# Attention on one core: values weighed one pair of units later, projections in the next group's first pairs, VectorE in another order

## What is computed

```python
def _L1_xattn_ref(x, context, Wq, Wk, Wv):
    q = x @ Wq.T
    k_raw = context @ Wk.T
    v_raw = context @ Wv.T
    ...
    q = _rmsnorm(q)
    k = _rmsnorm(k)
    scale = HEAD_DIM ** (-0.5)
    scores = jnp.einsum('bhnd,bhmd->bhnm', q, k) * scale
    attn = jax.nn.softmax(scores, axis=-1)
    out = jnp.einsum('bhnm,bhmd->bhnd', attn, v)
    return out.transpose(0, 2, 1, 3).reshape(b, n, NHEADS * HEAD_DIM)
...
x = x + jnp.tanh(g_xattn[1]) * _L1_xattn_ref(_layernorm(x, axis=-1), ctx_2048, L1_xattn_Wq, L1_xattn_Wk, L1_xattn_Wv)
x = x + jnp.tanh(g_ffn[1]) * _L1_ffn_ref(_layernorm(x, axis=-1), ...)
```

## Time and profile before

| | us |
|---|---|
| median of three runs (lowest, highest) | 1179.31 (1172.65, 1180.49) |
| the profiled execution, its own time | 1173.06 |
| its span, first to last instruction | 1171.2 |
| mean granted TensorE clock, share of full | 0.948 |
| PE busy | 984.8 |
| DVE busy | 695.1 |
| ACT busy | 670.7 |
| POOL busy | 505.5 |

### The profile page before, as it was taken

One profiled execution on the slowest core, in us unless ns is written; L12 is line 12 of the kernel. 1 busy time (PEld: TensorE's weight loads), 2 busy tenths in 40 slices (PEclk: granted clock), 3 DMA queues, 4 the chain that ended last, 5 costly groups with the idle time before them and its releaser, 6 DMA issues. The chain is left out here.

```text
span 1171.2 us, 27695 instructions
## 1 busy us (share of the span) xinstructions
PE 984.8 (84%) x9516; PEld 565.1 (48%) x9517; DVE 695.1 (59%) x1653; ACT 670.7 (57%) x1091; POOL 505.5 (43%) x442
## 2 busy tenths in 40 slices
PE   5889999969799799999879999974699898888840
PEld 2545656446576477776657777752122122111120
DVE  8686755578687453344333532214587787876677
ACT  4655655445343255565445644443778888899940
POOL 0222231157576345565545755542122354543422
PEclk9999999999899999999999999995899999999975
DMA  6534231389973377778676767657658889676211
GB/s 235 180 127 139 82 129 65 130 198 177 205 162 91 115 196 162 167 181 197 153 186 157 151 130 122 113 88 185 163 104 186 167 170 183 148 175 146 66 42 64
DMA packets 183636, 170.85 MB, mean 146 GB/s; under 512 B 137316, under 2 KB 138916, under 8 KB 182628
## 3 DMA queue, kind: packets, MB, share of 16 engines
q1 hardware_dynamic: 155698, 111.67, 38.4%
q0 software_dynamic: 25888, 56.43, 23.8%
q10 hardware_dynamic: 1954, 1.54, 0.5%
HBM read 80.87 MB, written 65.20 MB: 125 GB/s over the span
## 5 line engine op out<-in xcount | busy, mean ns | idle before, releaser
L2070 ACT ACTIVATE sb_atp<-ps_atpS 128x1024 f32<-128x1024 f32 x256 | 242.2, 1038 | 33.5 <-PE ps_atpS L1809 33.3
L1501 PEld LDWEIGHTS ps_shpH<-sb_roxT,sb_rowt 128*128 (+1 forms) x2844 | 169.0, 107 | 25.3 <-DVE sb_roxT L1361 6.7
L1501 PE MATMUL ps_shpH<-sb_roxT,sb_rowt 128*128 128x128 f16 (+1 forms) x2844 | 173.5, 220 | 6.4 <-DVE sb_roxT L1361 6.4
L1490 PE MATMUL ps_shpY<-sb_rowt,sb_rohhl 128*128 (+1 forms) x711 | 168.3, 382 | 0.5 <-DVE sb_rohhl L1366 0.4
L1821 PE MATMUL ps_atpO<-sb_atp,sb_atv 128*17 128x512 f32 x1024 | 135.6, 601 | 29.1 <-ACT sb_atp L2070 26.2
L1103 POOL DMA_INDIRECT sb_roxg<-xn,sb_roentry x79 | 81.8, 1036 | 122.1 <-DMA sb_roentry<-list 89.5
L1204 ACT ACTIVATE sb_roh<-ps_shpH,sb_rob 128x128 f32<-128x128 f32 (+1 forms) x237 | 68.9, 361 | 112.4 <-PE ps_shpH L1501 98.3
L1490 PEld LDWEIGHTS ps_shpY<-sb_rowt,sb_rohhl 128*128 128x128 f16 (+1 forms) x711 | 66.6, 98 | 67.6 <-issue 3.1
L1091 POOL DMA_INDIRECT list<-sb_shentry,sb_shposb x64 | 72.8, 1137 | 43.2 <-DVE sb_shposb L1276 26.3
L1193 ACT ACTIVATE sb_roy<-ps_shpY,sb_roentry 128x512 f32<-128x512 f32 x79 | 54.1, 685 | 65.2 <-PE ps_shpY L1490 45.6
L1113 POOL DMA_INDIRECT x2a<-sb_roy,sb_roentry x40 | 67.4, 1684 | 29.7 <-ACT sb_roy L1193 23.5
(11 more groups left out here) (354 smaller groups left out, 1769.7 us busy)
## 6 DMA issues: line engine op xcount, KB each, us to landing
sb_rowt<-rw SPq DMA_DIRECT2D x15, 768.0 KB
sb_rowt<-rw SPq DMA_DIRECT2D x15, 704.0 KB
kst<-sb_kykp SPq DMA_DIRECT2D x16, 512.0 KB
qst<-sb_quqp SPq DMA_DIRECT2D x12, 512.0 KB, 3.8
vst<-sb_kyvt SPq DMA_DIRECT2D x16, 272.0 KB
sb_atv<-vst SPq DMA_DIRECT2D x32, 136.0 KB
sb_stage<-ctxT SPq DMA_DIRECT2D x4, 1024.0 KB, 6.0
sb_shxin<-x SPq DMA_DIRECT2D x16, 256.0 KB
```

What stands on the lines that cost most here:

```text
L1490: last = e.matmul(pY[it.p][:, :], hhl[it.p][0:n, x, k * P:(k + 1) * P], weight(value, 2 * W1 + w + k * D, n, D), start=j == 0, stop=j == l ...
L1501: last = e.matmul(rpH[it.p][0:n, f * P:(f + 1) * P], weight(ex["up"], w + k * FF + f * P, P, n), rxT[it.p][:, x + k, :], start=j % (3 * KD ...
L2070: S.done(e.activation(pr[n % 6][:, :], pS[n % 3][:, :], ACT.Exp, scale=HD ** -0.5 / SA ** 2), "atexp")
```

## The change

The number of probability tiles `pr` goes from six to eight; the four tiles `xin`, which hold loaded rows before the first group, now lie in the first two `pr`, so that the SBUF used stays the same. TensorE weighs pair m-2 behind the scores of pair m, where it weighed pair m-1. A group's pairs 2 and 3 are therefore weighed in the next group, behind its scores of the pairs 0 and 1. Both halves of a projection now stand in group s+1, behind the scores of its pairs 0 and 1 and ahead of the `weigh` there. `turn` of the last group moves from behind `weigh` at pair 2 to ahead of `weigh` at pair 3. After the last group there are two `weigh` in place of one. On VectorE `projected`, `evacuate` and `normalise` move in each slot from behind `norm` to behind `choose` and `affine`, so that `scale`, `parts`, `spread`, `low`, `squares`, `scales` and `choose` of a slot come ahead of them; `roots` and `spread2` come behind them.

```diff
--- before.py
+++ after.py
@@ -1545,7 +1545,6 @@
         o = sb(mem, "o", [P, NT, D])
         x2 = sb(mem, "x2", [P, NT, D])
 
-        xin = [sb(mem, f"quxin{i}", [P, D]) for i in range(FIRST)]
         st, mv = [sb(mem, f"qust{i}", [P, 6]) for i in range(2)], [sb(mem, f"qumv{i}", [P, 2]) for i in range(2)]
         ve, rstd = ([sb(mem, f"qu{n}{i}", [P, 1]) for i in range(2)] for n in ("ve", "rstd"))
         rs = [sb(mem, f"qurs{i}", [P, 1]) for i in range(2)]
@@ -1562,7 +1561,9 @@
         q = [sb(mem, f"atq{i}", [P, 2, SEQ], f16) for i in range(3)]
         k = [sb(mem, f"atk{i}", [P, 2, SEQ], f16) for i in range(3)]
         vv = [sb(mem, f"atv{i}", [P, 4, 4 * (HD + 1)]) for i in range(3)]
-        pr = [sb(mem, f"atp{i}", [P, 2 * SEQ]) for i in range(6)]
+        NP_ = 8
+        pr = [sb(mem, f"atp{i}", [P, 2 * SEQ]) for i in range(NP_)]
+        xin = [pr[i // 2][:, i % 2 * D:(i % 2 + 1) * D] for i in range(FIRST)]
         oT = [sb(mem, f"atoT{i}", [P, SEQ]) for i in range(2)]
         rc = sb(mem, "atrc", [P, 4, 4])
         table = sb(mem, "attable", [P, 1])
@@ -1699,7 +1700,7 @@
                 r = slice(it.n * P, (it.n + 1) * P)
                 e.dma_start(x2[:, it.n, :], R["x2a"][r, :]).then_inc(S.sem(f"quxin{it.n}"), 16)
                 if it.n < FIRST:
-                    e.dma_start(xin[it.n][:, :], R["x1"][r, :]).then_inc(S.sem(f"quxin{it.n}"), 16)
+                    e.dma_start(xin[it.n], R["x1"][r, :]).then_inc(S.sem(f"quxin{it.n}"), 16)
 
             def turn(it):
                 S.reach(e, "quxl", it, it.n - FIRST + 1)
@@ -1819,7 +1820,7 @@
                 for i in range(4):
                     n = HD + 1
                     last = e.matmul(pO[it.p][32 * i:32 * i + n, :], vv[it.n % 3][:, m, i * n:(i + 1) * n],
-                                    pr[(it.n * 8 + 2 * m + i // 2) % 6][:, (i % 2) * SEQ:(i % 2 + 1) * SEQ], start=m == 0, stop=m == 3)
+                                    pr[(it.n * 8 + 2 * m + i // 2) % NP_][:, (i % 2) * SEQ:(i % 2 + 1) * SEQ], start=m == 0, stop=m == 3)
                 S.done(last, "atpv")
 
             def turn(it):
@@ -1873,17 +1874,16 @@
                     for m in range(4):
                         scores(it, 2 * m)
                         scores(it, 2 * m + 1)
-                        if m == 0 and it.n - 1 in started:
-                            project(started[it.n - 1], 6, 12)
-                        if m > 0:
-                            weigh(it, m - 1)
+                        if m < 2 and it.n - 1 in started:
+                            project(started[it.n - 1], 6 * m, 6 * m + 6)
+                        if m == 3 and it.n > 0:
+                            turn(it.back(1))
+                        if m > 1:
+                            weigh(it, m - 2)
                         elif it.n > 0:
-                            weigh(it.back(1), 3)
-                        if m == 2 and it.n > 0:
-                            turn(it.back(1))
-                        if m == 3 and it.n in started:
-                            project(started[it.n], 0, 6)
+                            weigh(it.back(1), m + 2)
                 if h == 2 * NG:
+                    weigh(It((NG - 1) // 2, 1), 2)
                     weigh(It((NG - 1) // 2, 1), 3)
                     turn(It((NG - 1) // 2, 1))
             e.wait_ge(S.sem("ato"), NG)
@@ -2065,9 +2065,9 @@
                 if n == 2:
                     for p in range(2):
                         S.wait_moved(e, "ququt", It(1, p))
-                if n >= 6:
-                    e.wait_ge(S.sem("atpv"), n // 2 - 2)
-                S.done(e.activation(pr[n % 6][:, :], pS[n % 3][:, :], ACT.Exp, scale=HD ** -0.5 / SA ** 2), "atexp")
+                if n >= NP_:
+                    e.wait_ge(S.sem("atpv"), (n - NP_) // 2 + 1)
+                S.done(e.activation(pr[n % NP_][:, :], pS[n % 3][:, :], ACT.Exp, scale=HD ** -0.5 / SA ** 2), "atexp")
 
             def signs(it):
                 S.wait(e, "law", it)
@@ -2151,7 +2151,7 @@
             def spread(it):
                 if it.n < FIRST:
                     v.wait_ge(S.sem(f"quxin{it.n}"), 32)
-                    line(v.tensor_tensor(x2[:, it.n, :], x2[:, it.n, :], xin[it.n][:, :], ALU.add))
+                    line(v.tensor_tensor(x2[:, it.n, :], x2[:, it.n, :], xin[it.n], ALU.add))
                 else:
                     v.wait_ge(S.sem(f"quxsum{it.n}"), 16)
                 line(v.bn_stats(st[it.p][:, :], x2[:, it.n, :]))
@@ -2329,12 +2329,6 @@
                         low(it)
                 for it in q_at(h, 2):
                     norm(it)
-                for it in g_at(h, 3):
-                    normalise(it)
-                for it in q_at(h, 6, FIRST):
-                    projected(it)
-                for it in g_at(h, 2):
-                    evacuate(it)
                 for it in n_at(h, 1):
                     scale(it)
                 for it in n_at(h, 2):
@@ -2345,19 +2339,25 @@
                     low(it)
                 for it in q_at(h, 7):
                     squares(it)
-                for i, at in n_slot.items():
-                    if at == h:
-                        roots(i)
                 for it in c_at(h, 2):
                     scales(it)
                 if h in inner_at:
                     chosen(inner_at[h])
                 for it in c_at(h, 4):
                     choose(it)
+                if h - 1 in inner_at:
+                    affine(inner_at[h - 1])
+                for it in q_at(h, 6, FIRST):
+                    projected(it)
+                for it in g_at(h, 2):
+                    evacuate(it)
+                for it in g_at(h, 3):
+                    normalise(it)
+                for i, at in n_slot.items():
+                    if at == h:
+                        roots(i)
                 for it in c_at(h, 1):
                     spread2(it)
-                if h - 1 in inner_at:
-                    affine(inner_at[h - 1])
                 if h - 2 in inner_at:
                     slices(inner_at[h - 2])
                 if h - 3 in inner_at:
```

## The result

| | before | after |
|---|---|---|
| median (lowest to highest), us | 1175.98 (1166.88 to 1180.49) | 1195.19 (1194.12 to 1197.45) |
| ratio, 95% interval | 1 | 1.015 (1.0114 to 1.0186) |
| profiled execution: span, us | 1171.2 | 1194.1 |
| mean granted TensorE clock | 0.948 | 0.933 |
| first to last exponential, us | 833.55 to 1116.34: 282.8 | 832.94 to 1139.04: 306.1 |

The changed kernel is 1.5% slower, some 19 us. The sum had said 4.4 us, so the side is right and the size is far off. The 1195.19 us lie above the forecast's own range (1175 to 1192) and just inside the wide one (1166 to 1196), and that is luck: the kernel before has a median of 1175.98 here and had 1179.31 in the forecast, where a ratio of 1.015 makes 1197.0. Within one per cent had the chance 0.61, and slower than that 0.23. All of the loss lies in the attention, which is 23.3 us longer in the profile.

What follows compares the result with a forecast made beforehand. TensorE was taken to bound groups with a projection, ScalarE the others. 1173.1 us less 15.7 of gains plus 20.1 of VectorE waits made 1177.5, or 1183.7 on the median's scale; range 1175 to 1192, eight in ten 1166 to 1196.

Steps and rivals of the forecast that it cites:

- The sum: Whole kernel: profiled 1173.1 us less 15.7 of gains plus 20.1 of losses, 4.4 us slower.
- Waits of groups 1 to 5: TensorE waits for `normalise` behind VectorE's new order in the early groups, together 10.8 us.
- The gain of 2.1 us: Groups 1 to 5: later weighing brings five groups to 9.50 us each, and group 1 starts 1.40 earlier.
- Groups 6 to 19: Two groups go from 18.01 to 17.1 us; late `normalise` costs waits of 1.5, 6.4 and 1.35 us.
- gains of 6.3 + 0.85: Middle groups: 0.9 us for each of seven pairs, 6.3, and a late transfer's 0.85 us counted as gone.
- about 1.5 of the signs': This stretch's part of the signs' waits for VectorE, 2.7 us in all, expected to go with `scales` earlier.
- Late groups: Groups 20 to 31, without projection: two take 15.22 us instead of 15.84, six pairs gain 3.7 us.
- The 0.22 and 0.98 gaps: ScalarE's usual idle gaps ahead of exponentials; their disappearance was named a sign of a right forecast.
- the gain of 15.7 us: Later weighing across the attention: gains of 3.7, 6.3, 2.7, 0.85 and 2.1 us together.
- A: Rival: VectorE is never late and the whole 15.7 us are gained, 1163.6 us; chance 0.18.
- B: Rival: TensorE's clock falls in the long waits for VectorE, 9.6 us more, 1193 us; chance 0.17.
- C: Rival: DMA engines bound the middle, bunching costs some 3 us, 1187 us; chance 0.05.

Runs made afterwards that it cites:

- e1: The changed kernel with the whole old order of steps on VectorE; 1185.21 us, ratio 1.0035 to the kernel before.
- e4: The changed kernel with `spread` alone moved behind `normalise` on VectorE; 1183.86 us, ratio 1.0037 to the kernel before.
- e12: The kernel of e6 without nine of the eleven steps of each `roots`; 1159.35 us, ratio 0.9938 to the kernel before.
- e9: The changed kernel with the old VectorE order, but `scales` ahead of `normalise`, and queries' transposes first in SyncE's queue; 1164.78 us, ratio 0.9983.
- e10: The kernel before, with its own weighing and six buffers, plus `scales` ahead of `normalise` and queries' transposes first in SyncE's queue; 1171.63 us, ratio 1.0057.
- e2: The changed kernel with `normalise` alone back in its old place behind `norm`; 1184.12 us, ratio 1.0043 to the kernel before.
- e5: The kernel of e2 with queries' transposes issued ahead of the rows' transposes and stores in SyncE's queue; 1172.51 us, ratio 1.0000 to the kernel before.
- e6: The kernel of e5 with `scales` ahead of `normalise` on VectorE; 1170.38 us, ratio 0.9970 to the kernel before.
- e8: The kernel of e6 with a group's values loaded behind its queries and counted by their own semaphore; 1172.74 us, ratio 0.9996 to the kernel before.

## Why the prediction was right or wrong

**Waits of groups 1 to 5: right.** Forecast 0.5, 2.5, 5.2, 2.1 and 0.5 us; in the trace 0.46, 2.60, 5.18, 2.01 and 0.58. The gain of 2.1 us is right as well: e1, which has none of these waits, takes 56.0 us for groups 0 to 5 and the kernel before 58.1. That groups 0 to 5 grew by 9.2 us, close to the sum's 10.8 - 2.1 = 8.7, is luck. The waits of 2.01 and 0.58 us lie behind the first exponential of group 6, so the sum had 6.1 us for this stretch; two falls of the clock in it (862.93 and 879.27) make 3.7 us of longer matmuls that it didn't have. Counting instructions start to start along VectorE's order gives waits to a tenth, where none of them waits for something else.

**Groups 6 to 19: the step that failed.** The sum had 9.25 us of new waits, and the 2.6 of group 5 besides, against gains of 6.3 + 0.85 and about 1.5 of the signs', so about 3 more; measured 17.3. Three terms were wrong. The largest is the clock: in this stretch the waits for VectorE are 3.5 us over the sum, the queries' 2.8 and the matmuls at half rate 8.3.

- `spread` was costed at its own 1.0 us. It also waits for its row, 1.8 to 1.9 us. Groups 9, 13 and 17 waited 1.33, 2.87 and 3.42 (forecast 1.35, 3.2, 3.2), but groups 11, 15 and 19, the light ones, 0.70, 2.25 and 1.43 instead of 0.4, 0.4 and 0.7. The waits of `spread` stand ahead of groups 11 and 15; ahead of group 19 there is no `spread` between `evacuate` and `normalise` (1031.52 to 1035.39), and why that one is twice its size stays open. The earlier trace rows show the step in a slot where its row had come. e4 confirms that the place counts: it alone was 13 us of the middle, more than half of it by the clock.
- The queries. The 0.85 us of a late transfer were counted as gone; they grew to 2.8 us of waits on TensorE. A shorter group wants its queries earlier, and they are issued no earlier.
- The clock. I made it a rival with 0.17, as in the earlier trace rows it fell only in a long stop. It fell six times in the attention behind waits. Against 1.47, 1.05 and 0.60 the rows at half rate are 12.0 us longer, which is more than the rival's 9.6. It should have been a term of the sum, as the same sum forecast waits of 2.5 to 5.2 us. The Trainium skill, TensorE: Matmul & The Clock Gate, "Part 1: The HAM clock gate", gives the two levels, and the trace agrees: 0.50 in the window 878 to 883.

**Late groups: right.** Two groups take 1080.82 - 1065.84 = 14.98 us (forecast 15.22, before 15.84 in the earlier trace rows), as 16 exponentials stand in one row now; the other pairs from group 20 on take 15.2 to 16.6 us, before 15.8 to 17.1. The stretch from group 20 on is 3.2 us shorter (3.7).

```profile
1065.84 14.74 ACT L2070 ACTIVATE sb_atp<-ps_atpS 128x1024 f32<-128x1024 f32 x16
1080.31 0.79 ACT L2075 ACTIVATE sb_lasg<-sb_law 128x512 f16<-128x512 f32 x1
1080.82 14.93 ACT L2070 ACTIVATE sb_atp<-ps_atpS 128x1024 f32<-128x1024 f32 x16
```

**The 0.22 and 0.98 gaps: half right.** The 0.22 are gone. Gaps of 0.7 to 1.0 us stand twice in a group with a projection, as the 0.72 and 0.98 of e12 above: there TensorE's rows follow on each other without idle time (905.22 to 914 us), so it is the bound of that stretch. The forecast had TensorE bound these groups too, so its sign that the 0.98 gaps would go contradicts its own sum.

**Is the gain of 15.7 us real?** In part it is shown. In the changed kernel 26.4 us of waits for VectorE or in front of a projection, 2.8 for queries and 12.0 at half rate, less 15.7, make 25.5; measured 23.3. In e12 TensorE waits 7.0 us for `evacuate` and loses 1.5 at half rate: 8.5 - 15.7 = -7.2; measured 275.1 - 282.8 = -7.7. That is an accounting with waits that partly cover each other, not a proof. The experiments for it are e9 against e10, 6.9 us, less than half of the 15.7, and e12's pairs of 17.09 us. e9 against e10 doesn't say either which part brings the 6.9 us: later weighing, the two more buffers or the projections' new places. What was wrong is to book the gain as if it came whole with the change. It needs queries, signs and copies that come earlier too, and each was just in time before. So the terms don't add: with the old VectorE order the change costs 0.35%, not -1.3%.

**Rivals.** A was not the case. The rule beside it, that repeated gaps can mean too few buffers (the Trainium skill, Perfetto Trace Analysis, "Optimization Strategy"), fits here in part: with eight buffers and later weighing the 0.22 gaps are closed but not the others, which waited for engines. B was right in its mechanism, and stood beside the forecast's own waits instead of in their place. C, as a floor of what e2 took, is refuted by e5: with the same transfers in another order 4.8 us went from the middle. Its bunching was real (shares of 0.34 and 0.99 in neighbouring windows of e2).

**What stays open.** The order that gets the whole gain was not found. e6 is the best that computes everything, 0.9970 (0.9939 to 1.0000), no more than a hint of a gain, and in it TensorE still waits 9.8 us for `evacuate` and 4.2 for `projected`. How much the steps of `roots` cost is open too: e12 is 8.0 us under e6 in the profiles and 0.3% by ratios whose intervals overlap.

## What to carry to other kernels

When steps move ahead of one that another engine waits for, cost them with their own waits (a load, another engine's result) and not only with their length; moving one such step took 1.1 of the 1.5% off here. When a change shortens the beat of a loop, write down for each transfer and side step when it is wanted now and when it was in time before: a gain is worth only what the next latest one allows, and its order in the issuing queue may need to change with it. Waits of 2 us and more on TensorE may cost twice, once as a wait and once at half rate behind it.

## What the runs showed of the hardware

The clock fell to 1.2 GHz behind waits shorter than the 2.6 to 5.2 us of rival B. In the changed kernel it fell behind waits of TensorE of 2.60, 5.18, 2.87, 2.25 and 3.42 us, and behind 1.95 + 0.70 us with one set of scores between them; in e1 behind 2.42, 2.56 and 2.72, each with a shorter one next to it; in e2 behind 2.35, and behind 1.30 + 0.52 (934.70, where a weighing takes 1.50 us, so before the wait of 1.97 for queries); in e12 behind 0.53 + 1.20 us with two short matmuls between them, and in e8 behind 0.53 + 1.18 in the same pattern. The window of e12 behind that last one:

```profile
957.00:959.00 2.00, 1.93 (x12) 0.87 (x12) 0.72 (x4) 1.18 (x2) 0.71 (x1) 0.50 1.01 233
```

It did not fall behind 2.01 us (905.57) in the changed kernel, nor in e1 behind 2.52 (898.57, where the half projection behind it takes the usual time), nor in e6 behind 1.18 with the same pattern as in e12. In e4 two waits of 2.50 us ended one way each:

```profile
966.61 2.70 PE L1846 MATMUL ps_atpO<-sb_rowt,sb_quxT 128*128 128x512 f16 x6 [2.50 <-DVE sb_o L2146]
...
1005.77 1.45 PE L1846 MATMUL ps_atpO<-sb_rowt,sb_quxT 128*128 128x512 f16 x6 [2.50 <-DVE sb_o L2146]
```

So between 1.2 and 2.5 us both happen, and the length of the wait alone doesn't decide. A fall cost 1.3 to 2.8 us of longer matmuls in the changed kernel.

TensorE's scores could start 7.8 us after the issue of their queries' DMA transposes when the DMA engines were in a burst: 928.93 to 936.77 in the kernel before (share 1.14 from 930 to 937 us) and 930.35 to 938.17 in e2 (1.03 from 925 to 935).
